# U of units 4 and 5 summed on GpSimd before TensorE streams it, with new tables of the schedule

## The reference

```python
s = q @ k.T                              # 1024 x 1024
s = s - s.mean(axis=-1, keepdims=True)
s = s / (abs(s).mean(axis=-1, keepdims=True) + 1e-6) * score_gain
r = maximum(where(causal, s, -1000.0), 0.0) ** 4
y = (r / (r.sum(axis=-1, keepdims=True) + 1e-6)) @ v
```

## Time and profile before

| | |
|---|---|
| median of 3 runs | 790.09 us (789.71 to 791.58) |
| the profiled execution: its own time, its span | 793.68 us, 792.0 us |
| mean granted TensorE clock | 0.956 of full speed |
| busy: TensorE, VectorE, ScalarE, GpSimd | 734.1, 680.8, 647.7, 543.4 us |
| DMA | 90.87 MB, 115 GB/s in the mean |

### The profile page before, as it was taken

One profiled execution on the slowest core, in us unless ns is written; L12 is line 12 of the kernel. 1 busy time (PEld: TensorE's weight loads), 2 busy tenths in 40 slices (PEclk: granted clock), 3 DMA queues, 4 the chain that ended last, 5 costly groups with the idle time before them and its releaser, 6 DMA issues.

```text
span 792.0 us, 17928 instructions
## 1 busy us (share of the span) xinstructions
PE 734.1 (93%) x5850; PEld 336.8 (43%) x5853; DVE 680.8 (86%) x1992; ACT 647.7 (82%) x1386; POOL 543.4 (69%) x552
## 2 busy tenths in 40 slices
PE   7869889889999999999999999999999999999986
PEld 6622222224444455445545444544544445442224
DVE  7679989899988987998898897889889898889982
ACT  4778988899988887898888987888888888889880
POOL 4016768765979687686948779594867969588760
PEclk9997887899999999999999999999999999999789
DMA  8876132155515542350445245044423614330586
GB/s 247 296 209 221 42 70 62 50 168 163 121 38 161 140 117 52 103 133 25 143 106 148 79 122 135 9 142 106 130 61 99 165 55 126 99 68 22 106 107 142
DMA packets 58350, 90.87 MB, mean 115 GB/s; under 512 B 8960, under 2 KB 41344, under 8 KB 58256
## 3 DMA queue, kind: packets, MB, share of 16 engines
q1 hardware_dynamic: 43200, 75.21, 34.4%
q0 software_dynamic: 10784, 12.53, 7.1%
q10 hardware_dynamic: 4272, 1.98, 0.9%
HBM read 61.29 MB, written 28.06 MB: 113 GB/s over the span
## 4 chain that ended last, share of the span: by engine, by line
PE 63%; ACT 12%; DVE 12%; issue 6%; POOL 6%; DMA 1%; another core or an unknown queue 0%; DVEq 0%; SPq 0%; ACTq 0%
PE bank L993 27%; PE bank L1028 8%; PE bank L1008 7%; PE bank L1069 7%; PE bank L1078 7%; DVE W L1339 5%; ACT U L845 5%; POOL W L690 4%; ACT W L866 3%; PE bank L1033 3%; DVE junk_V L1331 2%; POOL weighted_y L654 1%; PE bank L917 1%; DVE zT L1294 1%; PE bank L1024 1%
## 5 line engine op out<-in xcount | busy, mean ns | idle before, releaser
L993 PE MATMUL bank<-W,VS 128*10 128x512 f32 (+3 forms) x1536 | 300.8, 513 | 15.7 <-ACT W L866 9.6
L1339 DVE SCALAR_TENSOR_TENSOR W<-bank,U 128x512 f32<-128x512 f32 (+1 forms) x512 | 300.4, 649 | 14.0 <-ACT U L845 12.1
L993 PE MATMUL bank<-U,usel 128*10 128x512 f32 (+3 forms) x1536 | 297.2, 511 | 0.0
L845 ACT ACTIVATE U<-bank 128x512 f32<-128x512 f32 (+1 forms) x512 | 251.9, 590 | 43.9 <-PE bank L1078 41.4
L1331 DVE TENSOR_SCALAR_CACHE_REDUCE junk_V<-bank 128x512 bf16<-128x512 f32 (+3 forms) x508 | 228.8, 497 | 59.6 <-PE bank L1069 57.1
L690 POOL TENSOR_TENSOR W<-W 128x1024 f32<-128x1024 f32 (+3 forms) x174 | 261.9, 1516 | 15.8 <-DVE W L1339 5.5
L866 ACT ACTIVATE W<-W 128x1024 f32<-128x1024 f32 (+3 forms) x210 | 172.4, 858 | 3.3 <-POOL W L679 2.2
L679 POOL TENSOR_SCALAR_AFFINE_SELECT W<-W 128x512 f32<-128x512 f32 x127 | 81.6, 643 | 133.6 <-DVE W L1343 68.6
L1078 PE MATMUL bank<-QS,KS 48*128 48x512 bf16 (+3 forms) x768 | 137.3, 336 | 11.1 <-DVE W L1339 7.8
L837 ACT ACTIVATE junk_A<-bank 128x512 bf16<-128x512 f32 x132 | 74.5, 569 | 42.9 <-PE bank L1069 41.8
L1069 PE MATMUL bank<-KS,QS 48*128 48x512 bf16 (+3 forms) x640 | 95.7, 329 | 3.4 <-DVE parts L1275 1.6
(11 more groups left out here) (166 smaller groups left out, 659.3 us busy)
## 6 DMA issues: line engine op xcount, KB each, us to landing
wb<-in_experts SPq DMA_DIRECT2D x39, 707.0 KB
qk_parts<-parts SPq DMA_DIRECT2D x8, 768.0 KB, 6.1
KS<-qk_parts SPq DMA_DIRECT2D x192, 32.0 KB
QS<-qk_parts SPq DMA_DIRECT2D x192, 32.0 KB
xt_all<-sorted_x SPq DMA_DIRECT2D x39, 130.0 KB
sorted_x<-xt_all SPq DMA_DIRECT2D x3, 1300.0 KB, 12.2
xn_row<-weighted_y POOLq DMA_DIRECT2D x6, 512.0 KB, 6.5
v_stationary<-vb SPq DMA_DIRECT2D x4, 640.0 KB, 5.3
```

What stands on the lines that cost most here:

```text
L845: act.activation(U[n % NU][:, g, 0:w], score(n, k), ACT.Relu).then_inc(u_ready, 1)
L993: last = pe.matmul(acc[32 * g:32 * g + VW, lo:HALF], usel[:, :] if of_u else VS[q % 2][:, j, :, g], (U if of_u else W)[n % NU][:, g, 0:HAL ...
L1339: vec.scalar_tensor_tensor(W[n % NU][:, g, 0:w], score(n, k), 0.0, U[n % NU][:, g, 0:w], ALU.max, ALU.mult).then_inc(w_done, 1)
```

## The change

In quads 3 to 13 (PAIR_ENDS: the n of unit 5 in these quads; HELD: those and the ones before) GpSimd adds U of unit 4 to U of unit 5 in place, in two instructions of 128x1024 f32, once VectorE has made W of unit 5. TensorE streams neither in its own turn; in the turn of unit 6, behind the products of unit 6, it streams the sum. ScalarE waits for the additions before it writes U of unit 8 (slot of unit 4), and for one more count of used before U of unit 9 (slot of unit 5). The flags start and stop follow from what is now first and last.

The tables are redrawn with it: the kinds and engines of the pieces, the squares on GpSimd, the steps with two turns (TWICE) and without, the returns of rows, the steps of side tasks.

```diff
--- before.py
+++ after.py
@@ -79,7 +79,7 @@
             fits = [b for b in short if a[3] + b[3] == HALF]
             short.remove(fits[0])
             BY_HEAD[g].append([a, fits[0]])
-    ONE_PART = "1121122212212121121222111111"
+    ONE_PART = "1121222112112211111122211212"
     of_row = [[piece for g in (r, r + 2) for piece in BY_HEAD[g]] for r in range(2)]
     of_parts = {(r, k): [piece for piece in of_row[r] if (len(piece) == 1) == (k == "1")] for r in range(2) for k in "12"}
     PIECES = [of_parts[m % 2, k].pop(0) for m, k in enumerate(ONE_PART)]
@@ -87,9 +87,9 @@
     NP = len(PIECES)
     assert NP == sum(len(pieces) for pieces in BY_HEAD)
 
-    PLAN = ["VV", "VA", "VVAV", "AVVA", "V", "AV", "AV", "V", "V", "VV", "VVAV", "VAV"]
-    PLAN_EARLY = ["VV", "VA", "AVVV", "VVVA", "V", "VV", "VV", "V", "V", "VV", "VAVV", "VVA"]
-    PLAN_LATE = ["VV", "VA", "AVVV", "AVVA", "V", "VV", "AA", "V", "V", "VV", "VVAA", "AVV"]
+    PLAN = ["VV", "VA", "AVVV", "VAVV", "V", "VA", "V", "VV", "V", "VV", "VVAAV", "VV"]
+    PLAN_EARLY = ["VV", "VA", "VVVA", "VVAV", "V", "VV", "V", "VV", "V", "VV", "VVVAV", "AV"]
+    PLAN_LATE = ["VV", "AV", "VVAV", "VAVA", "V", "VV", "A", "VV", "V", "VV", "AVAVV", "AV"]
     EARLY, LATE = 3 * NS, ALL - NS
     plan = lambda n: (PLAN_EARLY if n < EARLY else PLAN if n < LATE else PLAN_LATE)[n % NS]
     PIECE_AT, PIECE_COUNT = [[] for _ in range(ALL)], [{"V": 0, "A": 0}]
@@ -102,11 +102,13 @@
     HEADS = [(1, 0, 3, 2) if (PIECE_AT[n][-1][0] % 2 == 0) else (0, 1, 2, 3) for n in range(ALL)]
     SCATTERS = TOPK * NT
     PER_STEP = 2
-    POOL_SQUARES = [(0, 1), (0,), (0, 1), (0,), (0, 1), (0,), (0,), (1,), (), (1,), (), (0,)]
-    POOL_EARLY = [(), (), (), (), (1,), (), (0,), (), (), (), (), ()]
-    POOL_LATE = [(1,), (0,), (), (1,), (0, 1), (0,), (1,), (), (0,), (1,), (), (0,)]
+    POOL_SQUARES = [(0, 1), (0,), (1,), (1,), (0, 1), (0,), (0,), (), (1,), (1,), (), (0, 1)]
+    POOL_EARLY = [(), (), (), (), (0,), (), (1,), (), (), (), (), ()]
+    POOL_LATE = [(0,), (0, 1), (1,), (), (0, 1), (0,), (0,), (), (0,), (), (1,), (1,)]
     by_pool = lambda n, p: p in (POOL_EARLY if n * PER_STEP < SCATTERS else POOL_SQUARES if n < LATE else POOL_LATE)[n % NS]
     NU, AVLAG = 4, 2
+    PAIR_ENDS = [q * NS + k for q in range(EARLY // NS, NQ - 2) for k in (5,)]
+    HELD = {b - i for b in PAIR_ENDS for i in range(2)}
 
 
     NXT, NWB, NYB = 6, 3, 4
@@ -116,15 +118,18 @@
     for p in range(NPAIR):
         TURNS += [("tx", p)] + [("m", i) for i in tiles_of(p)] + [("ga", p), ("gb", p), ("my", p)]
     FFN_FROM, FFN_TO = SCATTERS // PER_STEP + 3, ALL - 15
-    WITHOUT = [39, 47, 51, 59, 67, 71, 75, 79, 83, 95, 103, 107, 111, 115, 119, 131, 139, 143, 147, 151, 155, 167, 175]
-    FFN_AT, STEP_OF = [[] for _ in range(ALL + AVLAG + 2)], {}
-    for turn, n in zip(TURNS, [n for n in range(FFN_FROM, FFN_TO) if n not in WITHOUT], strict=True):
-        STEP_OF[turn] = n
-        FFN_AT[n].append(turn)
+    WITHOUT = [37, 38, 39, 46, 58, 63, 68, 70, 74, 75, 82, 94, 104, 106, 110, 111, 116, 118, 123, 130, 142, 146, 147, 152, 153, 154, 159, 166, 171]
+    TWICE = [50, 86, 100, 121, 136, 157]
+    FFN_AT, STEP_OF, left = [[] for _ in range(ALL + AVLAG + 2)], {}, list(TURNS)
+    for n in range(FFN_FROM, FFN_TO):
+        for _ in range((n not in WITHOUT) + (n in TWICE)):
+            FFN_AT[n].append(left.pop(0))
+            STEP_OF[FFN_AT[n][-1]] = n
+    assert not left
 
 
     ROWS, BACK_AT, due = -1, [[] for _ in range(ALL)], []
-    ROOM = [1, 0, 0, 0, 2, 2, 2, 1, 2, 0, 0, 0]
+    ROOM = [1, 0, 0, 1, 0, 0, 0, 1, 2, 2, 1, 2]
     for n in range(ALL):
         due += [(p, m) for kind, p in FFN_AT[n - 1] if n and kind == "my" for m in [ROWS, *range(2 * len(tiles_of(p)))]]
         while due and len(BACK_AT[n]) < (ROOM[n % NS] if n < FFN_TO - 2 else 2):
@@ -134,7 +139,7 @@
     NE = B - 1
     SIDE = [4 * NS * (b + 1) for b in range(NE)]
     BIAS_FROM = SCATTERS // PER_STEP + 6
-    S_SUMS, S_TURN, S_SCALE, S_SQUARE, S_ADD, S_TURNED, S_MOVE, S_TIMES, S_PROJ = 4, 6, 6, 7, 8, 9, 11, 16, 18
+    S_SUMS, S_TURN, S_SCALE, S_SQUARE, S_ADD, S_TURNED, S_MOVE, S_TIMES, S_PROJ = 4, 6, 6, 7, 8, 9, 11, 15, 19
     NSC = 6
     side = lambda n, by: [b for b in range(NE) if SIDE[b] + by == n]
 
@@ -149,7 +154,7 @@
         takers += [("proj", CH * b + c) for c in range(CH) for b in side(n, S_PROJ + c)]
     PLACE = {who: k for k, who in enumerate(takers)}
 
-    ADD_AT = [ALL - 10, ALL - 7, ALL - 6, ALL - 5, ALL - 4, ALL - 1]
+    ADD_AT = [ALL - 9, ALL - 7, ALL - 6, ALL - 5, ALL - 3, ALL - 1]
     ROUTE_M, ROUTE_PLACES, ROUTE_STEPS = 12, 24, 27
 
 
@@ -277,7 +282,7 @@
         qk_in = [sem("quad_in0"), sem("quad_in1")]
         s_ready, u_ready, w_done, w_mask = sem("scores_ready"), sem("u_ready"), sem("w_done"), sem("w_masked")
         r_ready = [sem(f"r_ready{i}") for i in range(NU)]
-        used = sem("u_and_r_used")
+        used, u_added = sem("u_and_r_used"), sem("u_of_two_units_added")
         acc_ev = sem("acc_evacuated")
         y_out, s_out = [sem("y_stored0"), sem("y_stored1")], [sem("sums_stored0"), sem("sums_stored1")]
         p_ready, p_used = sem("piece_ready"), {"V": sem("piece_used_vec"), "A": sem("piece_used_act")}
@@ -688,6 +693,11 @@
                             pool.wait_ge(w_done, 4 * n + 2 * p + 2)
                         some = slot[:, 2 * p:2 * p + 2, 0:w]
                         pool.tensor_tensor(some, some, some, ALU.mult).then_inc(r_ready[n % NU], 1)
+                if n in PAIR_ENDS:
+                    pool.wait_ge(w_done, 4 * (n + 1))
+                    for p in range(2):
+                        to, more = (U[m % NU][:, 2 * p:2 * p + 2, :] for m in (n, n - 1))
+                        pool.tensor_tensor(to, to, more, ALU.add).then_inc(u_added, 1)
                 if n >= BIAS_FROM and (n - BIAS_FROM) % 2 == 0 and (n - BIAS_FROM) // 2 < B:
                     x_and_bias((n - BIAS_FROM) // 2)
                 for b in side(n, S_SUMS):
@@ -839,7 +849,9 @@
                                 at += w
                             last.then_inc(p_used["A"], 1)
                     w = HALF - LOW[n % NS]
-                    wait(act, used, n - NU + 1)
+                    wait(act, used, n - NU + 1 + (n - NU in PAIR_ENDS))
+                    if n - NU + 1 in PAIR_ENDS:
+                        act.wait_ge(u_added, 2 * (PAIR_ENDS.index(n - NU + 1) + 1))
                     for k, g in enumerate(HEADS[n]) if not NARROW[n % NS] else ():
                         act.wait_ge(s_ready, 4 * n + k + 1)
                         act.activation(U[n % NU][:, g, 0:w], score(n, k), ACT.Relu).then_inc(u_ready, 1)
@@ -986,15 +998,14 @@
             less(3, 0, 1)
 
 
-            def average(n, p, of_u):
+            def average(n, p, of_u, start=False, stop=False):
                 q, (c, j), lo = n // NS, STEPS[n % NS], LOW[n % NS]
                 for r in range(2):
                     g = 2 * p + r
                     last = pe.matmul(acc[32 * g:32 * g + VW, lo:HALF],
                                      usel[:, :] if of_u else VS[q % 2][:, j, :, g],
                                      (U if of_u else W)[n % NU][:, g, 0:HALF - lo],
-                                     start=(j == 0 and of_u == bool(p)), stop=(n % NS in ENDS and of_u != bool(p)),
-                                     skip_group_check=True)
+                                     start=start, stop=stop, skip_group_check=True)
                 return last
 
             def ffn(kind, k):
@@ -1098,10 +1109,19 @@
                     pe.wait_ge(r_ready[y % NU], 2 * (y // NU + 1))
                     if STEPS[y % NS][1] == 0:
                         wait(pe, acc_ev, y // NS * CH + STEPS[y % NS][0])
-                    average(y, 0, False)
-                    average(y, 1, True)
-                    average(y, 0, True)
-                    average(y, 1, False).then_inc(used, 1)
+                    first, end = STEPS[y % NS][1] == 0, y % NS in ENDS
+                    if y - 1 in PAIR_ENDS:
+                        pe.wait_ge(u_added, 2 * (PAIR_ENDS.index(y - 1) + 1))
+                    of_u = [u for u in (y, y - 1) if (u in PAIR_ENDS if u < y else u not in HELD)]
+                    average(y, 0, False, start=first)
+                    if of_u:
+                        average(of_u[0], 1, True, start=first)
+                        average(of_u[0], 0, True, stop=end)
+                    last = average(y, 1, False, start=first and not of_u, stop=end)
+                    for u in of_u[1:]:
+                        average(u, 0, True)
+                        last = average(u, 1, True)
+                    last.then_inc(used, 1)
                 if n == ALL:
                     experts_of_last()
```

## The result

| | before | changed |
|---|---|---|
| median of 22 runs each | 791.43 us | 787.02 us |
| ratio | | 0.9943, 95% interval 0.9929 to 0.9957 |
| the profiled execution, its span | 793.7, 792.0 us | 788.8, 787.1 us |
| the same pair on a second chip (17 and 6 runs) | 782.46 us | 777.22 us, ratio 0.9928 (0.9910 to 0.9946) |

The account below looks back on a forecast made before the run. TensorE was taken to bound the turns' stage (quads 3 to 13, 98% busy). Pairs -9.4 and light quads +4.1 gave -5.3 us: 788.4 profiled, 784.8 against the 790.1 median; forecast 782 to 787.6, whole range 777 to 794.

Parts of the forecast that it names:

- The pairs' term: Quads 3 to 13: TensorE loses 0.85 us net a quad by fewer rounds, -9.4 us over 11 quads.
- The light quads: Quads 3, 6, 12 and 14, bound by VectorE, give back 4.1 us in sum (bounds 1 and 8).
- VectorE's work plus 2.1 us: Time of a quad bound by VectorE: 2.1 us above its work, bounds 1.1 and 3.1.
- Quads 3 and 12 near 43 and 42 us: Profile sign of being right: light quad 3 takes 43.0 us and quad 12 takes 42.3.
- counted at nothing: GpSimd's additions, placed in time in quad 7, are covered before ScalarE and TensorE need them: no cost.
- The additions themselves: Two GpSimd additions a quad at 2.36 us each, 4.7 us a quad (bounds 3.8 and 4.7).
- The size of the cover: Margin around the additions: 1.7 us for ScalarE, 0.6 or more for TensorE; if gone, ScalarE's relus of unit 8 wait.
- The turns: Quads 4, 7, 8, 11: weight loading needs 6.9 of 7.5 us, hidden; at most 0.6 us a quad, 2.4 in all.
- (a): Rival: the redrawn tables also close TensorE's idle time in the stage, 776 or 780.7 us; chance 0.20.
- (b): Rival: VectorE takes over in steps 4 to 7 of every quad, nothing gained, 790 give or take 2; chance 0.22.
- (c): Rival: lighter steps 6 and 7 make TensorE's clock fall in five more quads, +4.2 us, 794.3; chance 0.14.
- The rule from the Trainium skill: Beside (c): all eight quads without a clock fall would get one, 1.9 us each, and the kernel would end at 800.

Follow-up runs that it names:

- the two moves: Changed kernel with GpSimd's bias additions spread over quads 3 to 6 and the side task's first steps one later in quads 4, 8, 12: 773.4 us, ratio 0.9878.
- the tables alone: Changed kernel with all redrawn tables but no pair (PAIR_ENDS empty): 782.22 us, ratio 0.9998 against the kernel before.
- the extra 1.9: Changed kernel with one more 128x1024 GpSimd multiplication behind each pair, which ScalarE and TensorE also wait for: 791.18 us, ratio 1.0106 against before.
- the old returns: Changed kernel with only the table of returns of rows (ROOM) set back to that of before: 837.04 us, ratio 1.0693 against the kernel before.

## Why the prediction was right, and where it was not

- **The pairs' term** (-9.4): as work it was right. With the tables held TensorE's busy time in the stage fell by 9.4 us (484.5 to 475.1); rounds of W alone stay full; quad 7 gained 1.1 us. As time it was too large: with the tables held the pairs gave 5.5 us (3.7 to 7.3).
- **The light quads** (+4.1): the reasoning "VectorE's work plus 2.1 us" met quad 6 (43.0 for 42.6), quad 14 (40.9 for 40.3) and, with the two moves, quads 3 and 12. Light quads exist without the pairs too: with the tables alone TensorE idles for 2.9 us in quad 3 and 5.3 in quad 12, against 0.3 in quad 7. Yet the tables cost 0.0 +- 1.2 us in all, so something else in them pays for it; their executions were at half speed for 52 us in the mean, those of the kernel before on that chip for 57, which may be it and is not shown. Measured one by one, the two terms are thus -5.5 and 0.0 instead of -9.4 and +4.1: each is off by about 4 us, and the errors cancel. That the sum of -5.3 comes so near to 4.4 and 5.2 is in part luck.
- **"Quads 3 and 12 near 43 and 42 us"** failed, 48.1 and 44.1 (45.6 and 44.5 on the second chip, without a clock fall). Two different steps of the prediction were wrong. For quad 3 it is "counted at nothing", worked out for quad 7 alone: quad 3 has four additions of x and bias more in the same queue, and its step 11 took 5.5 us instead of the 3.8 it takes without one or the other. For quad 12 it is "2.1 us above VectorE's work": a load that a light step 5 (1.9 us) no longer covers comes on top, 2.6 us, with or without the pairs. The first was to be had from the trace of before, where the additions of x and bias (line 636 there) all lie between 185.6 and 231.0:

```profile
L636 POOL TENSOR_TENSOR xn_row<-xn_row,bp x4: 2186/2190/2204, 199.6 to 223.5; 128x1024 f32<-128x1024 f32 x4
```

- **The additions themselves** took 2.37 us each, as taken from line 641 of the kernel before (2.36).
- **The size of the cover.** The margins, 1.7 us for ScalarE and 0.6 or more for TensorE, were right to the size (0.6 us of the extra 1.9 were hidden), but what lies beyond was badly underrated. I wrote that ScalarE's relus would wait; the runs show 60 us for six returns a quad moved into steps 4 to 6. The price of a lost cover is not the lateness of one instruction: TensorE's order puts the next scores behind the late unit, the delay recurs in every quad, and of the 64 us by which the stage grew 25 are TensorE's own work at a lower clock.
- **The turns**: with the second m only two steps behind the my that frees its weights (7.5 us of TensorE's work by the prediction), the expert's weights came in time. In the stage of the changed kernel TensorE's weight loads waited twice for an expert's weights, 0.7 us in all (0.6 us with both moves), well inside the bound given.
- **Rivals.** (a) is not what happened, idle time rose. (b) not either: quads bound by TensorE gained what was taken off. (c): the clock fell in two quads of the stage (3 and 8) instead of three, and in none on the second chip. The rule from the Trainium skill that stood beside (c) ("TensorE: Matmul & The Clock Gate", A second HAM failure mode), that short idle spells between groups of matmuls make the gate go down and up, would have had it fall in every quad; the stage of the changed kernel on the second chip, with idle spells of up to 2.6 us and no fall, does not agree. With the old returns, where TensorE waited for 3.3 to 5.9 us in eight of the eleven quads and for 1.2 to 2.7 in the others, the clock fell in all eleven, and there the traces do agree.

## What to carry to other kernels

Work moved to an engine with a third of its time free can still cost: ask what stands ahead of it in that engine's order at that moment, and in every stage, not in the one quad looked at. This change pays only with a table that has nothing to do with it: the indirect DMAs that GpSimd issues at 1.3 us each are kept out of the steps around the additions; without that the kernel is 7% slower than before. A forecast that adds two large terms of opposite sign should be checked term by term, even when the sum comes true. And when a schedule has been balanced to within a microsecond, look for one-off side tasks (a bias, a load of sums) once its slack is gone.

## What the runs showed of the hardware that was not expected

On GpSimd the same tensor_tensor of 128x1024 f32 takes 1.89 us when it squares one tensor, 2.37 us when it adds two, and 2.18 us when the second is the bias repeated over its rows, and VectorE's products beside them did not get longer (group of line 1339: 649 ns in the mean before, 648 ns changed). With the old returns each wait of TensorE of 3.3 to 5.9 us, one in each of eight quads, had a fall of the granted clock to half, from 4.1 us before its end to 0.9 us behind it. Shorter waits decide nothing by themselves: with one more multiplication (up to 2.2 us) the clock fell in two quads of eleven, and a wait of 1.3 us in step 2 of quad 3 had such a fall in the first trace of the changed kernel and none in the second.
